# Bidirectional Mamba, layer norm and ternary FFN on one core: who multiplies by B and by C, and when the two ends of the passes do their work

## The reference, cut to what matters

```python
xi = silu(conv4(x @ in_proj_x)); z = x @ in_proj_z
dt, Bm, Cm = split(xi @ x_proj.T); dt = softplus(dt @ dt_w.T + dt_b)
dA = exp(dt[..., None] * A); dBx = (dt * xi)[..., None] * Bm[:, :, None, :]
h = dA * h + dBx; y = sum_s(h * C)      # a scan over time
y = (y + xi * D) * silu(z); out = y @ out_proj.T
```

## Time and profile before

| | us |
|---|---|
| median of three runs | 4865.73 (4864.23 to 4867.32) |
| the profiled execution | 4866.13 |
| its span, first to last instruction | 4864.3 |
| first scan starts | 76.90 |
| last unit of the passes scanned | about 3481 |
| first TensorE instruction of the FFN | 3543.30 |

### The profile page before, as it was taken

The page is one execution under the profiler, slowest core; times in us unless marked ns, Lnnn a source line. Parts: engine busy times, 40 slices in busy tenths (PEclk is TensorE's granted clock), DMA queues, the critical chain, the costliest instruction groups (busy, mean ns, idle before and its releaser), DMA issues. The chain is left out here.

```text
span 4864.3 us, 61578 instructions
## 1 busy us (share of the span) xinstructions
PE 4310.0 (89%) x22500; PEld 3152.6 (65%) x22500; DVE 4006.5 (82%) x4251; ACT 3249.3 (67%) x5210; POOL 3436.0 (71%) x1599
## 2 busy tenths in 40 slices
PE   8888888888888888888888888887689999999999
PEld 3555555566555556656555665565578888888888
DVE  6999999999999999999999999999844444445452
ACT  7777777777777777777777777777344444444443
POOL 5999999999999999999999999999600000000000
PEclk9999999999999999999999999999889999999999
DMA  7433333333333333333333333334130101010100
GB/s 262 139 124 121 118 113 113 116 115 121 116 112 117 121 111 122 114 114 109 118 114 109 112 113 120 111 108 152 57 117 31 35 31 35 31 35 31 32 25 9
DMA packets 176418, 474.96 MB, mean 98 GB/s; under 512 B 15024, under 2 KB 99376, under 8 KB 141488
## 3 DMA queue, kind: packets, MB, share of 16 engines
q1 hardware_dynamic: 175216, 459.44, 28.0%
q10 hardware_dynamic: 896, 11.54, 0.8%
HBM read 435.27 MB, written 47.19 MB: 99 GB/s over the span
## 5 line engine op out<-in xcount | busy, mean ns | idle before, releaser
L1244 DVE TENSOR_TENSOR_SCAN m_h<-bank,m_state,m_dBx 128x512 f32<-128x512 f32 x1792 | 2181.9, 1263 | 34.8 <-ACT bank L1033 29.1
L772 PEld LDWEIGHTS bank<-ident,m_h 128*128 128x128 f32 x8192 | 1010.3, 147 | 653.1 <-issue 332.7
L772 PE MATMUL bank<-ident,m_h 128*128 128x128 f32 x8192 | 1246.5, 284 | 165.6 <-DVE m_h L1253 104.4
L1140 POOL TENSOR_TENSOR m_dBx<-u,m_Bs 128x1024 f32<-128x1024 f32 x512 | 1202.8, 2388 | 3.1 <-DVE m_h L1276 1.2
L1140 POOL TENSOR_TENSOR m_dBx<-m_u,m_Bs 128x1024 f32<-128x1024 f32 x512 | 1200.5, 2377 | 2.1
L1253 DVE TENSOR_TENSOR m_h<-m_h,bank 128x1024 f32<-128x1024 f32 x736 | 880.4, 1196 | 27.7 <-PE bank L754 24.2
L1033 ACT ACTIVATE bank<-m_dt,cols 128x512 f32<-128x512 f32 x1024 | 691.4, 688 | 247.0 <-DVE m_h L1244 243.6
L1033 ACT ACTIVATE bank<-dt,cols 128x512 f32<-128x512 f32 x1024 | 690.4, 688 | 204.7 <-DVE m_h L1244 201.5
L754 PEld LDWEIGHTS bank<-ident,m_Ct 128*128 128x128 f32 x2944 | 346.5, 143 | 676.3 <-DVE m_h L1253 456.9
L754 PE MATMUL bank<-ident,m_Ct 128*128 128x128 f32 x2944 | 486.3, 290 | 315.0 <-DVE m_h L1253 312.6
L292 POOL TENSOR_TENSOR mvj<-mvj,norm_c 128x4 f32<-128x4 f32 x16 | 16.2, 1015 | 1058.3 <-DVE mvj L253 1058.3
(11 more groups left out here) (169 smaller groups left out, 5198.4 us busy)
## 6 DMA issues: line engine op xcount, KB each, us to landing
m_Bs<-b_dram SPq DMA_DIRECT2D x256, 1024.0 KB, 4.8
m_Cs<-c_dram SPq DMA_DIRECT2D x288, 256.0 KB, 3.2
xx<-in_x SPq DMA_DIRECT2D x16, 512.0 KB, 7.2
xn_dram<-xx SPq DMA_DIRECT2D x16, 512.0 KB, 4.4
yb_dram<-m_ysb SPq DMA_DIRECT2D x16, 512.0 KB, 6.8
xx<-xn_dram SPq DMA_DIRECT2D x16, 512.0 KB, 3.9
x_dram<-m_ysb SPq DMA_DIRECT2D x16, 512.0 KB, 6.8
base<-xn_dram SPq DMA_DIRECT2D x16, 512.0 KB, 3.9
```

The lines of the kernel that those rows point to most:

```text
L772: mm = pe.matmul(YB[b][:, o:o + P], h[:, k % NH, m, tok:tok + P], ident[:, :], start=(s == 0 and o == 0), stop=False, is_transpose=True, s ...
L1140: pool.tensor_tensor(dBx[:, k % NDBX, :, :], u[ch.batch][:, m, :], Bs[:, k // BP % 2, k % BP, :].unsqueeze(1).broadcast_to((P, 2, T)), ALU ...
L1244: dve.tensor_tensor_scan(h[:, k % NH, m, flip(ch)], DA[ch.at(STEPS, i) % NDA][:, flip(ch)], dBx[:, k % NDBX, m, flip(ch)], initial, ALU.mu ...
```

## The change

- `A_UNITS` = 18, 21, 24, 27 and 30 no longer have a product by GpSimd. TensorE transposes u's blocks 2 and 3 once a chunk (`turn_u`, half-slots 26 and 29; ScalarE copies the result out, `keep_uT`), and for each of the five units it multiplies that by diagonal matrices of B, four products a block, straight into a `DA` bank (`fill_a`, half-slots 2k-2 and 2k-1). ScalarE writes the decays of these units into `h` instead, and the scan runs in place.
- The diagonal matrices come from HBM: `store_b` writes B's elements one by one onto the diagonals of zeroed matrices in `d_dram` (four DMAs of 640 elements), and `load_d` loads 256 KB for each unit.
- `P_UNITS` grows from nine to twelve units, so VectorE and `spread_c` have 20 where they had 23.
- OUT moves to half-slots 32 to 35 and 38 to 41.
- Prologue: the Z jobs of chunk 0 move to half-slots 33, 46, 38 and 52, the last casts and sums to earlier ones; ten DMAs of 256 KB zero `d_dram`.
- Last chunk: the modulation rows are made by TensorE in it (`rows`, seven jobs) and copied by ScalarE. Flush: GpSimd computes batch 0's gains and `make_base`; batch 1's gains and the FFN's come in the FFN's block; VectorE only joins, gates and norms.

```diff
-      J_Y: (46, 47, 13, 17), J_OUT: (29, 35)}
+      J_Y: (46, 47, 13, 17), J_OUT: (32, 38), J_UT: (26, 29)}
+FIRST_Z = (33, 46, 38, 52)
+AT_ROWS = (16, 21, 26, 30, 32, 37, 41)
-P_UNITS = (1, 5, 7, 9, 13, 15, 17, 21, 25)
+P_UNITS = (1, 5, 7, 9, 12, 14, 16, 17, 19, 21, 24, 26)
+A_FIRST, A_STEP, NA = 18, 3, 5
-CAST_AT = (4, 7, 9, 13, 17, 22, 30, 35, 38, 43, 50)
-SUM_AT = (10, 10, 18, 18, 27, 28, 33, 36, 41, 46, 52)
+CAST_AT = (4, 7, 9, 13, 17, 22, 30, 35, 38, 40, 43)
+SUM_AT = (10, 10, 18, 18, 27, 28, 33, 36, 41, 43, 48)
...
+                for n in range(TS):
+                    sp.dma_start(by_diagonal[:, :, n * P], dbB[s:s + A_STEP * (NA - 1) + 1:A_STEP, n * P:(n + 1) * P],
+                                 allow_slow_non_contiguous=True).then_inc(S["b_st"], 16)
...
+            def fill_a(ch, g):
+
+                for i, k in enumerate(A_UNITS):
+                    m = g - (2 * k - 2)
+                    if not 0 <= m < 2:
+                        continue
+                    n, tile = ch.at(NA, i), ch.at(STEPS, 2 * k + m)
+                    if m == 0:
+                        if i == 0:
+                            wait_drained(pe, ch, J_UT[1])
+                        pe.wait_ge(d_in[n % NDG], 16 * (n // NDG) + 16)
+                    pe.wait_ge(S["scan"], tile - NDA + 1)
+                    for s in range(TS):
+                        mm = pe.matmul(DA[tile % NDA][:, s * P:(s + 1) * P], uT[:, s, m * P:(m + 1) * P],
+                                       dg[:, n % NDG, s, :], start=True, stop=True)
+                    mm.then_inc(S["a_fill"], 1)
...
                         for m in range(2):
                             turn_y(ch, g, m)
+                            turn_u(ch, g, m)
+                        fill_a(ch, g)
                         if has(ch, 1):
                             front(ch.go(1), g)
+                        else:
+                            rows(g)
...
+                if k in A_UNITS:
+                    dve.wait_ge(S["a_fill"], ch.at(2 * NA, 2 * A_UNITS.index(k) + m + 1))
+                    decays, share = o, da
+                else:
+                    decays, share = da, dBx[:, dbx_ring(ch, k) % NDBX, m, flip(ch)]
+                dve.tensor_tensor_scan(o, decays, share, initial, ALU.mult, ALU.add).then_inc(S["scan"], 1)
```

More of the change, by code:

```diff
@@ L393, in count, with before @@
                 return sum(BANK[k] == b for k in jobs)
-            def before(jobs):
-                return sum(BANK[k] == b and START[k] < START[i] for k in jobs)
+            def before(jobs, start=START):
+                return sum(BANK[k] == b and start[k] < start[i] for k in jobs)
             nf, nm, nt = count(FRONT), count(MID), count(TAIL)
@@ L410, in job, with row_job @@
                 off = -nt + before(TAIL)
-            return b, ch.at(nf + nm + nt, off - back * (nf + nm + nt))
+            return b, ch.at(nf + nm + nt, off - back * (nf + nm + nt) + more)
+        def row_job(e):
+            last = Chunk(NPASS - 1, NC - 1, 1)
+            return job(last, next(i for i in MID if BANK[i] == R_BANK))[1] - len(AT_ROWS) + e
         def wait_filled(eng, ch, i):
@@ L627, in body @@
                     store_xn(ch.go(2))
+                load_d(ch, 2)
+                load_c(ch, 8)
                 if has(ch, 1):
@@ L1555, in _ @@
         def _(pool):
+            pool.wait_ge(SM["lng_in"], 64 + 48)
+            for k in range(KM):
+                pool.sem_inc(S["go"], 1)
+                wait_filled(pool, Chunk(0, 0, 0), F_LN + k)
+            scratch = [xn[:, i, :] for i in range(3)]
+            gains = Gains(pool, SM, Gains.BRANCH)
+            gains.branch(1, gain, ot, *scratch)
+            gains.ffn(0, gain, ot, *scratch)
+            gains.ffn(1, gain, ot, *scratch)
             for n in range(1, NCH):
@@ L1594, in body @@
                     rest(ch, X_H1 + m, F_H1 + m, gb[:, :, m, :])
-                    if not ch.last():
-                        J.join(dve, ch.go(1), m)
-                        norm(ch.go(1), m - 4)
+                    if ch.first() and m == 0:
+                        dve.wait_ge(SM["gain_p"], 2 * Gains.BRANCH)
+                        for step in range(3):
+                            J.make_base(dve, ch.go(1), step)
+                    elif not ch.last():
+                        first = 1 if ch.first() else 0
+                        J.join(dve, ch.go(1), m - first)
+                        norm(ch.go(1), m - first - 4)
                 if not ch.last():
@@ L1614, in _ @@
             norm_rest(Chunk(0, 0, 0))
-            for step in range(3):
-                J.make_base(dve, Chunk(0, 0, 1), step)
             schedule(dve, body)
```

299 lines of the change are left out of this document (191 added, 108 removed).

## The result

The changed kernel takes 4925.8 us (median of four runs, 4924.65 to 4928.23) against 4866.5 for the kernel before (four runs too): a ratio of 1.0123, 95% interval 1.0108 to 1.0138. It is 59 us **slower**. The forecast was 4860, within 4685 to 4895; neither its sign nor its range holds.

The account below looks back on a forecast made before the run. VectorE (98% busy) and GpSimd (99%) were taken to bound the passes. Against 4866.1 us: ordinary chunks +32, chunks 16 and 17 -2, start through chunk 1 -9, flush -29, FFN +1, so -7, about 4860; range 4685 to 4895.

Parts of the forecast that it names:

- The fill wait: Slots 16 to 20: walking TensorE's in-order work, VectorE starts unit 21's second scan at 20.9, not 15.3; 5.7 us a chunk.
- the rival at 0.19: Fills: each instruction costs 0.19 us instead of 0.109, adding 70 us over 27 chunks, 4930 in all; chance 0.08.
- There are 27 of them: Passes: ordinary chunks, 2 to 14 and 18 to 31, each take the net +1.2 us, +32 together.
- The sum: Whole kernel: the predicted gains and losses added up to -7 us, about 4860; the near break-even case, chance 0.50.
- What the wait absorbs: Ordinary chunk: the fill wait hides 0.8 us for `spread_c` after slot 20 and 0.4 of ScalarE's table loads in slot 31.
- +1.2 a chunk: Ordinary chunk: -3.3 for VectorE's products, -0.8 and -0.4 for absorbed waits, +5.7 for the fill wait, in us.
- I take zero: DMA queues: the 2560 single elements ahead of `load_b` 6 add no time beyond latency, so no stall.
- the 18 at the other end: DMA queues: upper limit for the element stores if all is work, 10 x 1.8 us, stalling GpSimd by 4.
- this rival: Unit 25: element stores make GpSimd late by 4 us a chunk, +120, 4980; decides from 14 us on; chance 0.14.
- GpSimd stays late: 0: Chunk 15: GpSimd also makes the second pass's diagonals and remains the late engine, so its length changes by 0.
- The ends: Prologue: first scan near 72.7, not 76.90, chunk 2 earlier by 9 in all; flush: -29; FFN: +1, in us.
- 0.28 of the 0.47 for a gain: Passes: two faster cases, no wait in slots 16 to 20 (4690 us, chance 0.18) and half of it (4790, 0.10).

Follow-up runs that it names:

- Experiment 4: Also spelled fill_half: the changed kernel with two of the four products of each bank's fill left out; 4930.5 us, ratio 1.0136.
- Experiment 3: The changed kernel with OUT moved from half-slots 32 and 38 to 38 and 44; 4997.0 us, ratio 1.0273.
- half_no_elements: The changed kernel without the element stores and with two of four products of each bank left out; 4858.1 us, ratio 0.9981.
- no_elements: Also experiment 1: the changed kernel without the four element stores a chunk, all loads, fills and scans kept; 4910.8 us, ratio 1.0095.
- elements_late: The changed kernel with the element stores moved from ahead of load_b 6 to behind load_c 10; 4909.9 us, ratio 1.0089.
- experiment 6: Also ends_only: the kernel before with only the change's rebuilt prologue, last chunk and flush; 4837.6 us, ratio 0.9938.
- experiment 9: The changed kernel with the element stores late, as in elements_late, and GpSimd's last unit 25 instead of 26; 4899.9 us, ratio 1.0069.
- experiment 7: The same run as elements_late: the changed kernel with only the four element stores moved behind load_c 10; 4909.9 us, ratio 1.0089.

## Why the prediction was wrong, point by point

**The fill wait.** Right in place and size: 6.0 a chunk in slots 17 to 21, ahead of scans of units 18 and 21 or just behind, against 5.7 (20.9 - 15.3 of the walk are 5.6); a bank 0.89 against 0.87. Experiment 4 shows that it is the length of the fills (1.8 for half of four banks, at 0.11 an instruction), so the rival at 0.19 is out. Experiment 3 shows that it isn't OUT's place alone.

**Where the wait applies.** This step failed: "There are 27 of them". The sum gave chunks 0, 1, 15, 16 and 17 no fill wait, because GpSimd was the late engine there before. But the change relieves GpSimd, and TensorE's order is the same in every chunk that has one before it: chunks 1, 15, 16 and 17 wait 5.8 to 6.0 in these slots too, where they waited 1.0 to 1.3 before, with 3.3 of removed products to set against it. That it is the fills there as well, half_no_elements shows against no_elements: chunk 1 is 2.8 shorter, chunks 16 and 17 together 2.1. Of the 9.5 missed in chunks 16 and 17 this is the larger part; 2.4 are the stores' (elements_late). Of the 11.4 missed up to chunk 2, 3.9 are the stores' and some 3.5 the prologue's, of whose 4.2 0.7 is left (experiment 6); the other 4 are for the most part chunk 1's, 2.4 longer than before in elements_late too.

Chunk 0 is another case. It has no OUT of a chunk before it, and half the fills don't shorten it (105.0 against 104.7). Its 4.9 for the fill in slot 21 fell on a stretch in which TensorE was at its lower clock, 1.2 GHz, for most of the time; columns as in the earlier trace rows:

```profile
138.00:142.00 4.00, 3.64 (x14) 2.57 (x14) 3.69 (x4) 0.16 (x1) 4.00 (x3) 0.61 0.71 237
142.00:146.00 4.00, 4.00 (x18) 3.35 (x18) 0.08 (x1) 2.34 (x5) 4.00 (x3) 0.53 0.82 34
```
In elements_late the granted clock is 1.00 in both stretches, and the wait there is 1.8. What sets the clock here is open.

**What the wait absorbs.** The 0.8 behind `spread_c` went as forecast (24.2 us in front of L1400 before, 5.9 after). The 0.4 in slot 31 did not: that wait is 0.7 before and after. With 0.35 more for the fills and 0.4 of small waits in slots 27, 30 and 31 this makes an ordinary chunk of elements_late some 1.1 longer than the sum, 29 us over 27 chunks. This is the largest part of the miss: +1.2 a chunk was the sum, +2.2 came in elements_late, +2.6 in the changed kernel.

**The element stores.** "I take zero" failed; the 18 at the other end was too much. They cost 9.3 - 4.8 = 4.5 behind them in the DMA queues and 4.65 of SyncE's issue time, 9 in all (by the landing of `load_b` 6, 81.6 after a chunk's start for 73.5 in elements_late, it is 8.1), under the 14 from which I let this rival decide. What I left out is that GpSimd comes late to units 25 and 26 already at 9: it stands still for 6 us in every chunk, and slot 25 waits 0.5. The kernel paid in chunk 0 (3.5, in slots 21 and 25), in ordinary chunks (0.3 each) and in 16 and 17. Together 4925.8 - 4909.9 = 16. The Trainium skill's rule on small transfers ("DMA: Bandwidth & Descriptors", section "Specifications"), that below 512 B the engines read, modify and write, pointed the right way: the engines are busy and move 0 to 3 GB/s, though no run shows what they are busy with. The Trainium skill's rule of five engines (same page, section "Why a DMA increments its semaphore by 16 and not by 1") can't be settled here. Five of 16 would be a busy share of 0.31 and the slices above average over 0.4, but that share adds up packet times of which several can run at once, and the profile doesn't name the engine of a packet.

**Chunk 15.** "GpSimd stays late: 0" failed, by 6.5. GpSimd enters the chunk with a lead of 3.0 instead of 7.3, and 9.3 of diagonals in four slots take all of it: slots 0 to 3 last 20.4, for 16.1 before. One part is the place of its last unit (1.8, shown by experiment 9); the fill wait that is now in this chunk as well is another: 6.0 in slots 17 to 21, for 1.0 before, against 3.3 of removed products.

**The ends.** The flush was right: -28.4 alone and -27.0 in the change, against -29; the prologue's 4.2 were not, for GpSimd's first product began only 0.8 earlier; the FFN +0.1 against +1.

**The whole.** The misses by the table: 11.4 + 37.1 + 6.5 + 9.5 + 2.0 - 0.9 = 65.6, and 4860 + 65.6 = 4925.6. Of the 37.1 in ordinary chunks 8.5 are the stores', 28.6 the sum for one chunk (its fill wait 0.35 short, slot 31's 0.4 not absorbed, and small waits left out). So three steps failed where it counts: the +1.2 for an ordinary chunk (29 us), no fill wait outside the 27 chunks, and zero for the element stores (16 us in all). The gain of the prologue and the 0 of chunk 15 are smaller misses. The forecast stood near break-even by a sum of one gain and one wait of about the same size, so small errors in every chunk set its sign; and 0.28 of the 0.47 for a gain rested on mean busy shares that the in-order sum already spoke against. No case was held for "the sum, but in all chunks".

## What to carry to other kernels

A wait that comes from one engine's written order applies in every turn of the loop that has the same work, also in those that another engine bounded before: put it in all of them, then ask whose lead is left. When two paths bound a kernel at nearly the same length, removing one can show nothing (fill_half: +5 against the changed kernel; no_elements: -15; both: -68), so test them together before calling a cost harmless. Work given to an engine that has room on average belongs in the slots where nothing waits for it: with the same ends, five units from 18 on lose 88 us against ends_only, and three from 24 on, with the stores moved and GpSimd's units chosen anew, win 47. How much of that is the place and how much the smaller number, no run shows.

## What the runs showed that I had not expected

- Four stores of 640 single elements each took SyncE's queue for 4.65 us and the DMA engines for about 5.6, and cost nothing at another place in the queue (experiments 1 and 7: 4910.8 and 4909.9).
- Moving one load ahead of them made the kernel 32 us slower, since the next load in line had less time to spare than the one that was saved.
- Taking a product from VectorE in slot 15 gained 0.4 of its 1.1 us in an ordinary chunk and nothing in all, in slot 27 0.9 and 22 us in all (4812.7 and 4790.9, from 4813.1): by the trace a decay behind ScalarE's table loads sets the length of slot 15.
- TensorE's lower clock lay in the middle of chunk 0's longest wait for a fill (granted 0.53 to 0.61), and the same stretch at full clock waited 3.1 us less.
